# Ranking twelve token tiles in one block, other orders around it, and the experts' second bias added by VectorE

## The reference, cut to what matters

```python
x = x + tanh(g_xattn[0]) * cross_attention(layernorm(x), ctx, ctx, mask, Wq, bq, Wk, bk, Wv, bv, Wo, bo)
xt = layernorm(x)                                       # 2048 tokens x 256
S = sigmoid(xt @ Wg)                                    # 8 experts
G, I = top_k(S, 2)
h = gelu(einsum('nd,edf->enf', xt, W1) + b1[:, None, :])   # 256 -> 1024
y = einsum('enf,efd->end', h, W2) + b2[:, None, :]         # 1024 -> 256
x = x + tanh(g_ffn[0]) * sum over the two chosen experts of G * y
```

## Time and profile before

| what | value |
|---|---|
| median of 3 runs | 477.69 us (476.35 to 482.83) |
| the profiled execution: its time | 476.38 us |
| the profiled execution: its span | 474.6 us |
| PE busy | 402.5 us (85% of the span) |
| DVE busy | 304.2 us (64%) |
| ACT busy | 226.8 us (48%) |
| POOL busy | 176.7 us (37%) |
| the product for b2 (L1333) | 39 instructions |
| scatters (L467) | 39 instructions |

### The profile page before, as it was taken

The page is one execution under the profiler, slowest core; times in us unless marked ns, Lnnn a source line. Parts: engine busy times, 40 slices in busy tenths (PEclk is TensorE's granted clock), DMA queues, the critical chain, the costliest instruction groups (busy, mean ns, idle before and its releaser), DMA issues.

```text
span 474.6 us, 11156 instructions
## 1 busy us (share of the span) xinstructions
PE 402.5 (85%) x4056; PEld 318.9 (67%) x4056; DVE 304.2 (64%) x819; ACT 226.8 (48%) x577; POOL 176.7 (37%) x194
## 2 busy tenths in 40 slices
PE   5757988898989879872199999999999999999980
PEld 3632445455555445452189999999999999999970
DVE  4757787878877686867646656556555656565640
ACT  2343765655656557447054444444444444444420
POOL 8735532313222132110233444444444444444231
PEclk9965899999999999896579999999999999999996
DMA  7563444624554354312011223322222233332221
GB/s 220 111 177 112 122 141 127 218 97 120 153 155 121 100 178 123 106 45 49 19 42 35 48 47 56 56 51 47 48 46 48 47 50 53 54 49 42 33 24 22
DMA packets 35702, 40.25 MB, mean 85 GB/s; under 512 B 10982, under 2 KB 30306, under 8 KB 35650
## 3 DMA queue, kind: packets, MB, share of 16 engines
q0 software_dynamic: 12608, 27.48, 25.7%
q1 hardware_dynamic: 20497, 11.18, 8.5%
q10 hardware_dynamic: 2544, 0.88, 0.8%
HBM read 25.86 MB, written 9.50 MB: 75 GB/s over the span
## 4 chain that ended last, share of the span: by engine, by line
PE 65%; DVE 17%; DMA 7%; issue 4%; ACT 4%; POOL 2%; POOLq 0%; ACTq 0%; SPq 0%; DVEq 0%
PE bank L1318 7%; PE bank L1320 7%; PE bank L1319 7%; PE bank L1335 7%; PE bank L1334 7%; PE bank L1336 7%; PE bank L1063 4%; DMA out_rows<-y_sb,scatter_tab 4%; PE bank L1080 3%; DVE rowmax L734 3%; PE bank L1250 3%; PE bank L1101 3%; PE bank L1282 2%; DVE W L800 2%; PE bank L1223 1%
## 5 line engine op out<-in xcount | busy, mean ns | idle before, releaser
L1318 PE MATMUL bank<-xh,W 128*128 128x128 f16 x624 | 121.8, 221 | 0.9 <-DVE xl L975 0.9
L1319 PE MATMUL bank<-xl,W 128*128 128x128 f16 x624 | 121.8, 221 | 0.0
L1320 PE MATMUL bank<-xh,W 128*128 128x128 f16 x624 | 121.7, 221 | 0.0
L659 ACT ACTIVATE h<-bank,b1T 128x128 f32<-128x128 f32 x312 | 88.9, 368 | 62.3 <-PE bank L1320 59.7
L467 POOL DMA_INDIRECT out_rows<-y_sb,scatter_tab x39 | 61.8, 1585 | 112.7 <-DVE y_sb L993 103.7
L1334 PE MATMUL bank<-W,hh 128*128 x312 | 85.1, 273 | 1.0 <-DVE hl L986 1.0
L1336 PE MATMUL bank<-W,hl 128*128 x312 | 85.0, 273 | 0.0
L1335 PE MATMUL bank<-W,hh 128*128 x312 | 85.0, 273 | 0.0
L984 DVE CAST hh<-h 128x512 f16<-128x512 f32 x78 | 34.2, 439 | 63.5 <-ACT h L659 63.5
L734 DVE TENSOR_REDUCE rowmax<-bank 128x2 f32<-128x308 f32 x128 | 57.1, 471 | 25.8 <-PE bank L1080 24.7
L1318 PEld LDWEIGHTS bank<-xh,W 128*128 x624 | 61.7, 99 | 4.3 <-DVE xl L975 1.3
(11 more groups left out here) (185 smaller groups left out, 669.7 us busy)
## 6 DMA issues: line engine op xcount, KB each, us to landing
W_stage<-in_L_ffn_W POOLq DMA_DIRECT2D x32, 512.0 KB, 4.2
xn_scratch<-attn SPq DMA_DIRECT2D x8, 256.0 KB, 2.2
qst<-qh SPq DMA_DIRECT2D x60, 32.0 KB, 2.5
X_late<-in_x SPq DMA_DIRECT2D x6, 256.0 KB, 6.8
out_rows<-X_late SPq DMA_DIRECT2D x6, 256.0 KB, 2.5
qst<-ql SPq DMA_DIRECT2D x28, 32.0 KB, 2.8
xg<-xn_scratch,gather_tab POOLq DMA_INDIRECT x39, 2.9
out_rows<-y_sb,scatter_tab POOLq DMA_INDIRECT x39, 3.8
```

Of the source, the lines that this page charges most:

```text
L659: ins = nc.scalar.activation(h32[s % 4][:, m * P:(m + 1) * P], H_BANKS[s % 4][:, m * P:(m + 1) * P], ACT.Gelu_apprx_tanh, scale=1.0 / W_SC ...
L1318: nc.tensor.matmul(dst, wh, xh[t % 3][:, cut], start=(c == 0), stop=False)
L1319: nc.tensor.matmul(dst, wh, xl[t % 3][:, cut], start=False, stop=False)
L1320: ins = nc.tensor.matmul(dst, wl, xh[t % 3][:, cut], start=False, stop=(c == KC - 1))
```

## The change

1. **Ranking.** FIRST and SECOND become one group EARLY of twelve tiles, ranked once on DVE in frame 7, i = 4, where SECOND was. Only the clearing of `ahead` and `chosen16` stays in frame 6. The number of groups goes from four to three (`chosen_made`, `gates_made`, `gates_stored` count to three).
2. **Frame 8 on PE.** Before: turns of unit 7's values, turns of unit 6's normalised rows, counts of EARLY, logits of unit 6. Now: normalised rows, values, logits, and the counts of EARLY in i = 5, between the turns for Wo and the product with Wo.
3. **Frame 8 on DVE.** The marks of the first six tiles go from i = 4 to i = 6, behind the residual of unit 7; those of the next six from i = 6 to i = 8. The four marks of NEXT go behind `rank_experts(LATE)`.
4. **The second bias.** b2's halves, `b2x`, its zeroing, the 16 transfers and the product are gone. SP loads b2 in fp32, spread over all partitions (8 KB each, 1 MB in all), in frame 8. `weigh_y` is now two operations: y = b2 row x 64 + bank, then y = y x gate, with a semaphore between them; the row is chosen by a register of DVE, loaded eight tiles at a time.
5. **The end.** `weigh_y` follows LAST_LEAD from step 69 on: tiles 33, 34 and 35 are weighed one step earlier than before, tile 37 before the last `split_h` and not behind it.

```diff
@@ setup, SP, POOL, ACT @@
-                if u == 0:
-                    sp.wait_ge(b2_zeroed, 1)
-                    sp.wait_ge(b2_made, 1)
-                    for v, row in enumerate((0, B2_LOW_ROW)):
-                        for e in range(E):
-                            sp.dma_start(b2x[row:row + 1, e, :].bitcast(F16), b2_pair[e:e + 1, v, :]).then_inc(b2_landed, 16)
+                if u == U:
+                    sp.wait_ge(pv_done, ITEMS * U)
+                    sp.dma_start(b2_rows[:, :, :].rearrange("p e d -> p (e d)"), b2.rearrange("e d -> (e d)").partition_broadcast(P)).then_inc(b2_loaded, 16)
...
-            nc.gpsimd.memset(b2x[:, :, :].bitcast(F32), 0.0).then_inc(b2_zeroed, 1)
-            pool.wait_ge(b2_zeroed, 1)
...
-            act.dma_start(b2_stage[:, :], b2).then_inc(b2_loaded, 16)
...
@@ DVE, frames @@
-                        dve.wait_ge(q_free, q_nth["logits", U - 4])
-                        rank_experts(FIRST)
                     if u == U - 1 and i == 4:
                         dve.wait_ge(q_free, q_nth["logits", U - 3])
-                        rank_experts(SECOND)
+                        rank_experts(EARLY)
...
                         find_places(EARLY)
+                    if u == U and i == 6:
                         mark_tokens(0, slice(0, EARLY.stop // 2))
-                    if u == U and i == 6:
+                    if u == U and i == 8:
                         mark_tokens(0, slice(EARLY.stop // 2, EARLY.stop))
-                    if u == U and i == 8:
                         dve.wait_ge(ranked, 2)
                         find_places(NEXT)
-                        mark_tokens(0, NEXT)
-                        mark_tokens(1, NEXT).then_inc(first_marked, 1)
 
             dve.wait_ge(q_free, len(Q_USES))
             rank_experts(LATE)
+            mark_tokens(0, NEXT)
+            mark_tokens(1, NEXT).then_inc(first_marked, 1)
...
@@ DVE, experts @@
             def weigh_y(t):
+                e = dve.snap(dve_expert[t], min_val=0, max_val=E - 1)
+                row = b2_rows[:, bass.ds(e, 1), :].rearrange("p o d -> p (o d)")
+                dve.lower_ap(row)
                 dve.wait_ge(h_used, 2 * t + 2)
                 dve.wait_ge(gate_picked, t + 1)
                 if t >= 3:
                     dve.wait_ge(scattered, 16 * (t - 2))
-                nc.vector.tensor_scalar(y_sb[t % 3][:, :], Y_BANKS[t % 2][:, 0:D], gate_tab[:, t:t + 1], None, ALU.mult).then_inc(y_made, 1)
-
+                nc.vector.scalar_tensor_tensor(out=y_sb[t % 3][:, :], in0=row, scalar=W_SCALE, in1=Y_BANKS[t % 2][:, 0:D],
+                                               op0=ALU.mult, op1=ALU.add).then_inc(y_biased, 1)
+                dve.wait_ge(y_biased, t + 1)
+                nc.vector.tensor_scalar(y_sb[t % 3][:, :], y_sb[t % 3][:, :], gate_tab[:, t:t + 1], None, ALU.mult).then_inc(y_made, 1)
...
             for s in range(2 * NT):
                 if s % 2 == 0 and s // 2 + 1 < NT:
                     to_low(s // 2 + 1)
-                if s % 2 == 1 and 5 <= s < 2 * NT - 1:
-                    weigh_y((s - 5) // 2)
+                while 2 * done + (LEAD if s <= CATCH_UP else LAST_LEAD) + 2 <= s and done < NT - 2:
+                    weigh_y(done)
+                    done += 1
+                if s % (2 * EXPERTS_PER_LOAD) == 2 * EXPERTS_PER_LOAD - 1 and s // 2 + 1 < TAB:
+                    load_experts(s // 2 + 1)
+                split_h(s)
                 if s == 2 * NT - 2:
-                    weigh_y(NT - 3)
-                split_h(s)
-            weigh_y(NT - 2)
+                    weigh_y(NT - 2)
             weigh_y(NT - 1)
@@ PE @@
-                    if u == U and i == 0:
-                        pe.wait_ge(rowmax_done, 2 * NPAIR * U)
-                        pe.wait_ge(pv_evac, 2 * U)
-                        for j in range(2):
-                            turn_values(j, LAST_TURN[j]).then_inc(last_turned, 1)
...
                     if u == U and i == 0:
-                        pe.wait_ge(consts2_made, 3)
-                        pe.wait_ge(exp_done, ITEMS * U)
-                        pe.wait_ge(chosen_made, 2)
-                        count_places(EARLY, first=True)
+                        pe.wait_ge(rowmax_done, 2 * NPAIR * U)
+                        pe.wait_ge(pv_evac, 2 * U)
+                        for j in range(2):
+                            turn_values(j, LAST_TURN[j]).then_inc(last_turned, 1)
...
+                    if u == U and i == 5:
+                        pe.wait_ge(consts2_made, 3)
+                        pe.wait_ge(exp_done, ITEMS * U)
+                        pe.wait_ge(chosen_made, 1)
+                        count_places(EARLY, first=True)
...
-                if m == 0:
-                    nc.tensor.matmul(y, b2_rows[:, :], row, start=True, stop=False)
-                nc.tensor.matmul(y, hh[s % 4][:, cut], both[0], start=False, stop=False)
+                nc.tensor.matmul(y, hh[s % 4][:, cut], both[0], start=(m == 0), stop=False)
```

More of the change, by code:

```diff
@@ L237, in build @@
         q_nth = {use: n + 1 for n, use in enumerate(Q_USES)}
-        FIRST, SECOND, NEXT, LATE = (slice(a, b) for a, b in ((0, T - 6), (T - 6, T - 4), (T - 4, T - 2), (T - 2, T)))
-        EARLY = slice(0, SECOND.stop)
+        EARLY, NEXT, LATE = slice(0, T - 4), slice(T - 4, T - 2), slice(T - 2, T)
         LAST_TURN = bank[6:8]
@@ L346, in _ @@
                     send_query(u + 3)
-            for n, tiles in enumerate((FIRST, SECOND, NEXT, LATE)):
+            for n, tiles in enumerate((EARLY, NEXT, LATE)):
                 sp.wait_ge(gates_made, n + 1)
@@ L595, in _ @@
                         weights_high(3)
-                    if u == 0 and i == 2:
-                        act.wait_ge(b2_loaded, 16)
-                        nc.scalar.activation(b2_pair[:, 0, :], b2_stage[:, :], ACT.Copy, scale=W_SCALE).then_inc(b2_high, 1)
                     if i == 0 and live(u - 1):
@@ L1119, in count_places @@
                     nc.tensor.matmul(bank[0][:, 0:b * E], before[:, :], chosen16[:, 0:b * E], start=True, stop=False, skip_group_check=True)
-                    nc.tensor.matmul(bank[2][:, b * E:T * E], before[:, :], chosen16[:, b * E:T * E], start=True, stop=False, skip_group_check=True)
+                    for t in (NEXT.start, LATE.start):
+                        nc.tensor.matmul(bank[2][:, t * E:(t + 2) * E], before[:, :], chosen16[:, LATE.start * E:T * E], start=True, stop=False, skip_group_check=True)
                 else:
@@ L1322, in layer1, with layer2 @@
                     ins.then_inc(h_filled, 1)
-            def layer2(t, m, both, row):
+            def layer2(t, m, both):
                 s = 2 * t + m // (FC // 2)
@@ L1363, in _ @@
                     if h >= 0:
-                        row = b2_at(expert[t2]) if m2 == 0 else None
                         both = w2_at(expert[t2], m2)
@@ L1367, in _ @@
                     if h >= 0:
-                        layer2(t2, m2, both, row)
+                        layer2(t2, m2, both)
                     if m == 2 and t + 1 < NT:
```

43 lines of the change are left out of this document (16 added, 27 removed).

## The result

| | before | changed |
|---|---|---|
| median, four runs each on one chip | 479.18 us (476.35 to 482.83) | 474.07 us (473.35 to 475.69) |
| profiled execution: time, span | 476.38 us, 474.6 us | 474.62 us, 472.5 us |
| span from the first expert product to the start of the last scatter | 227.74 us | 222.35 us |

The ratio is 0.9892, 95% interval [0.9847, 0.9937]: about 1.1% faster, inside the 2% that I called no change. The forecast of 470.0 us (467.3 to 472.6) was too low. The predicted structure is there, but the time is not.

What follows compares the result with a forecast made beforehand. PE without gaps was taken to bound the expert tiles, a chain across engines the routing, scatter landings the end; 4.1 + 1.2 + 1.5 = 6.8 us off 476.38 us, plus 0.4 us, gave 470.0 us (467.3 to 472.6).

Steps and rivals of the forecast that it cites:

- Expert tiles, 4.1 us: Expert tiles: 37 products for b2 of 0.11 us leave PE; DVE's 0.45 us longer weighing hides in its gelu wait.
- The end, 1.2 us: Last scatters: tiles 33 to 35 weighed one step earlier, so the last scatters start 1.2 us earlier.
- Routing, 2.4 - 0.9 = 1.5 us: Frames 8 and 9: the new order gives 2.4 us, NEXT's four marks behind the last ranking cost 0.9 us.
- Each time on the old scale: Frames 8 and 9, in the earlier trace's times: unit 7's residual at 212.2 us, LATE's ranking 221.15, tile counts 224.75.
- The low half that I put at 1.13 us: Frame 7 on DVE: 1.13 us for the low half before the ranking, putting unit 6's residual at 200.45 us.
- the slow clock in frame 8: Rival: clock falls after PE's 2.1 us gap before 204.1 us, leaving about 0.3 us of routing's gain; 471.2 us, chance 0.28.
- I take 0; bounds 0 and 1 us: Setup: removing sixteen transfers, five short DVE and ACT operations and a memset gains 0, at most 1 us.
- The sentence on the earlier trace: Frames 1 to 5: PE waits once or twice in each, yet the clock stays full; used against a slow clock.
- For a median I add 0.4 us: Whole kernel: 0.4 us added to 469.6 us, as the profiled execution was at the lowest of the runs shown.

Runs made afterwards that it cites:

- bias_only: Against the kernel before, only the second bias changed (part 4), the weighings left where they were; 473.18 us, ratio 0.9889.
- order_only: Against the kernel before, only parts 1 to 3 (ranking and the orders of frame 8), the second bias still a product; 477.77 us, ratio 0.9969.
- after: The changed kernel with all five parts, first measurement and profile; median 474.07 us, profiled execution 474.62 us, ratio 0.9892.
- after_again: The changed kernel run and profiled once more, nothing altered; 473.71 us, ratio 0.9894 to the kernel before.

## Why the prediction was wrong

1. **Expert tiles, 4.1 us: right.** The tile period fell by 0.11 us and tile 38's low half came 3.9 us earlier behind the first product in `bias_only` (206.77, not 210.66 us). DVE's second operation was covered. 3.5 us reached the last scatter: in `bias_only` the scatters behind tile 35's were 4.6 to 4.8 us apart, not 4.5 to 4.7 us.
2. **The end, 1.2 us: right**, 1.5 us. The two terms together: 5.3 us forecast, 5.0 us by the means (227.6 less 222.65 us).
3. **Routing, 2.4 - 0.9 = 1.5 us: the events right, the worth unsettled.** Each time on the old scale was met within 0.7 us, and the marks cost 0.8 us. (The low half that I put at 1.13 us takes 1.23 us in the earlier trace rows; unit 6's residual still came at 200.3 us, forecast 200.45.) But it is a gain against a first profile in which the clock had fallen at 196 us. wo5 to the experts is 57.5 us on the mean of eleven profiles with the new order (57.1 to 58.4) and 58.1 us on that of four with the old (57.3 to 58.9; the two long ones had the fall). By time `order_only` gives 1.5 us, interval 0.2 to 2.7 us. My rival, the slow clock in frame 8, came true in the profile (0.60 from 211 to 217 us); it took less than I gave it.
4. **The setup, "I take 0; bounds 0 and 1 us": this step failed.** I priced the removed instructions by their work and their queue, and let that exclude a loss. Four fewer on DVE moved its stream: the reciprocal that became number 321 met a hole of 0.26 us, where a new block of instructions begins, PE's wait in frame 5 grew from 1.34 us past the longest of frames 1 to 5 (1.59 us, frame 1), and the clock fell behind it: 1.4 us on the mean, up to 2.0 us. The sentence on the earlier trace rows, that PE waits there too and the clock stays full, was true of one execution only: behind frame 1's 1.59 us, which that execution had as well, the clock fell in seven of twenty profiles. So the profile of the change carries, besides the hole, 1.3 us of a fall that the base had missed by luck.
5. **"For a median I add 0.4 us": too little.** The median of before in the runs of the result was 479.18 us, 2.8 us above the profiled execution.

From 479.2 us: less 3.5, 1.5 and 1.5 (order, by time), plus 1.4, is 474.1 us, against 474.07 us measured; without the order's 1.5 us, which its interval nearly allows, it would be 475.6 us. Against my 470.0 us, 2.4 us are the base and 1.4 us the hole. That this closes so well is partly luck: the same terms give 476.8 us for `bias_only`, which measured 473.18 us, and the changed kernel itself was 5.1, 5.2, 6.3 and 7.9 us under before in its four comparisons. What I took from the Trainium skill, "TensorE: Matmul & The Clock Gate", Part 1, was that slow products at a start differ between runs of one kernel. The trace agrees: the first stretch at half clock (0.50) lasted from 31.5 to 52.0 us in `after` and from 28.4 to 52.3 us in `after_again`. But the spread that counted was not at a start: it was falls behind waits in the middle, and a kernel's runs spread over 2 to 10 us (the one run of 802.86 us left out).

## What to carry to other kernels

A sum of removed and added work is good to a few tenths where PE has no gap, and not in stretches with gaps near the point where the clock falls: there a delay of a third of a microsecond cost four to six times as much in the seven profiles of nine in which the clock fell behind it. Before an edit of the setup is priced at nothing, look for waits of PE that a small shift would lengthen and for the instruction of DVE that begins a block ahead of them, and profile the base more than once: a wait behind which the clock stayed full in one execution can see it fall in the next. Where TensorE must wait between two phases, idle products sized to end before the wait bought 4.2 us here; where the first group was longer and met a slow clock, half of that was lost again.

## What was not expected of the hardware

- DVE stood still for 0.26 us at instruction 321, or 193, of its stream, when the one before it was a wait: in all ten profiles with such a pair there, and in none of the ten others. A division at number 193, without a wait ahead, was 0.10 us late in nine of nine. Behind each of these a packet of 8192 bytes of instructions starts within 0.8 us.
- The clock's fall does not follow from the length of a wait alone: behind 2.1 us in frame 7 it fell in two of the four profiles with the old order; behind 1.70 us in eight of ten; behind 1.59 us in frame 1 in seven of twenty; behind 1.34 us in frame 5 in none of eleven. It came within 2 us of the wait's end or some 10 us later.
